# Row-tiled attention scores and maxima on 32 partitions, with another division of the PSUM banks

## The reference

```python
x = x + L0_ffn(L0_cond(x, cond))      # 8 experts of 3 layers, top 2; then attention with 16 heads
                                      # of 4 channels, and 8 experts of 2 layers, top 2
x = x + L1_ffn(L1_cond(x, cond))      # attention with 16 heads of 8 channels; then 16 experts
                                      # with a capacity of 160 rows each, top 2

# the attention of either layer (hd = 4, then 8)
scores = einsum("bhsk,bhtk->bhst", Q, K) / sqrt(hd)
attn = softmax(scores, axis=-1)       # over 512 keys, for each of 16 heads and 512 queries
ao = einsum("bhst,bhtv->bhsv", attn, V)
```

## Time and profile before

| What | Value |
|---|---|
| Median of 3 runs (range) | 543.95 us (543.36 to 544.02) |
| Profiled execution, span | 541.2 us |
| Profiled execution, own time | not listed beside its span; the median is 2.75 us above the span |
| VectorE busy | 315.8 us (58%), 826 instructions |
| ScalarE busy | 278.7 us (51%), 414 instructions |
| GpSimd busy | 136.3 us (25%), 136 instructions |
| Experts A | from about 14 to 136 us |
| Loop of layer 0, first scores to the last values | from 136.4 to about 256 us |
| Loop of layer 1 | from 329.3 to about 456 us |

### The profile page before, as it was taken

How to read it: one execution, slowest core, us unless ns; L and a number is a source line. 1 busy time by engine, 2 the same in 40 slices (tenths; PEclk the granted TensorE clock), 3 DMA queues, 4 the chain that set the end, 5 groups by cost and what they waited for, 6 DMA issues and landing times.

```text
span 541.2 us, 7612 instructions
## 1 busy us (share of the span) xinstructions
PE 494.7 (91%) x2782; PEld 345.1 (64%) x2782; DVE 315.8 (58%) x826; ACT 278.7 (51%) x414; POOL 136.3 (25%) x136
## 2 busy tenths in 40 slices
PE   5899799998989999999999988999999999889980
PEld 4578678886545555554897865445555554669970
DVE  4654444567778787764263577877788663402223
ACT  6734344552546566667454653556656555205640
POOL 5755622331711101200000000101111005231551
PEclk9999899999999999999999998999999999899995
DMA  8970200000700000020000000000000002540003
GB/s 323 303 234 2 78 1 0 1 1 1 307 5 0 1 2 0 1 79 0 2 1 0 1 2 1 1 0 1 0 1 2 0 1 94 249 107 4 19 18 120
DMA packets 12868, 26.57 MB, mean 49 GB/s; under 512 B 1293, under 2 KB 10120, under 8 KB 11808
## 3 DMA queue, kind: packets, MB, share of 16 engines
q1 hardware_dynamic: 11392, 22.91, 12.5%
q0 software_dynamic: 1440, 3.18, 1.9%
HBM read 22.11 MB, written 5.26 MB: 51 GB/s over the span
## 4 chain that ended last, share of the span: by engine, by line
PE 77%; DVE 10%; ACT 5%; issue 3%; DMA 3%; POOL 2%; POOLq 0%; DVEq 0%; SPq 0%; ACTq 0%
PE PS L436 13%; PE PS L468 11%; PE PS L453 10%; PE PS L690 5%; PE PS L579 5%; PE PS L613 5%; PE PS L581 5%; PE PS L580 5%; PE PS L730 3%; PE PS L721 3%; DVE mx L1153 3%; PE PS L342 3%; PE PS L421 2%; PE PS L422 1%; PE PS L443 1%
## 5 line engine op out<-in xcount | busy, mean ns | idle before, releaser
L1153 DVE TENSOR_REDUCE mx<-PS 128x1 f32<-128x512 f32 x256 | 164.6, 685 | 41.8 <-PE PS L436 39.3
L854 ACT ACTIVATE wc_late<-PS 128x1024 f32<-128x1024 f32 x128 | 123.9, 1022 | 62.2 <-PE PS L453 62.0
L436 PE MATMUL PS<-Kp,Qs 128*128 128x512 f32 x256 | 95.9, 438 | 6.9 <-DVE mx L1153 5.2
L436 PEld LDWEIGHTS PS<-Kp,Qs 128*128 128x128 f32 x256 | 44.7, 190 | 70.4 <-DVE mx L1153 40.3
L453 PE MATMUL PS<-Qm,Kp 128*128 128x512 f32 x256 | 75.2, 415 | 0.8 <-DVE Qm L1165 0.6
L468 PE MATMUL PS<-wc_late,v_c 128*16 128x512 f32 x512 | 67.3, 598 | 0.7 <-ACT wc_late L854 0.7
L1438 POOL CAST Kp<-Ks 32x512 fp32r<-32x512 f32 x40 | 24.3, 607 | 135.0 <-ACT Ks L833 133.1
L453 PEld LDWEIGHTS PS<-Qm,Kp 128*128 128x128 f32 x256 | 46.5, 190 | 18.1 <-ACT wc_late L854 3.8
L579 PE MATMUL PS<-wc_late_r 128*128 128x512 f32 x96 | 41.7, 435 | 1.1 <-POOL xT_yT_r L1400 0.6
L1052 DVE TENSOR_SCALAR work<-PS,early 128x512 f32<-128x512 f32 x32 | 22.6, 747 | 25.1 <-PE PS L581 25.1
L954 ACT ACTIVATE work<-PS,late 128x160 f32<-128x160 f32 x64 | 19.8, 396 | 32.5 <-PE PS L721 32.5
(11 more groups left out here) (244 smaller groups left out, 743.5 us busy)
## 6 DMA issues: line engine op xcount, KB each, us to landing
wa<-wa_dram SPq DMA_DIRECT2D x8, 512.0 KB, 9.0
wa<-wc_dram SPq DMA_DIRECT2D x2, 2048.0 KB, 9.8
wc_late<-wc_dram SPq DMA_DIRECT2D x2, 2048.0 KB, 11.1
wb<-wb_dram SPq DMA_DIRECT2D x1, 2048.0 KB, 15.6
sel<-sel_dram POOLq DMA_DIRECT2D x2, 1024.0 KB, 5.6
late<-late_dram SPq DMA_DIRECT2D x1, 1572.0 KB, 14.9
packed_rows<-ao SPq DMA_DIRECT2D x1, 1290.0 KB, 22.9
wb<-packed_rows SPq DMA_DIRECT2D x5, 258.0 KB, 4.3
```

The lines of the kernel that those rows point to most:

```text
L436: filled(mm(p, Qs[:, G % 3, qt * P:(qt + 1) * P], Kp[:, G % 3, j, :], start=True, stop=True), (L, "max", G, qt, j))
L854: A(E4[:, 2 * (i % 2) + jp, :, :], p, ACT.Exp, scale=float(HD[L]) ** -0.5).then_inc(taken[f"s{jp}"], 1)
L1153: V.reduce_max(mx[:, G % 2, qt, j:j + 1], p, AX.X).then_inc(taken[filled_at[key][0]], 1)
```

## The change

Scores and maxima are computed on row tiles of the array: a matmul reads only the 32 partitions of its head's slice, of keys and of queries, with `tile_position=(SL * j, 0)`. So the padded keys `Kp` go, with their clearing, with `place_keys` on GpSimd, with ScalarE's four slices, and with the waits on `Kp_set`. One `Ks` with three buffers takes their place, written by one instruction of ScalarE in every group.

The PSUM slots of the loop change. The maxima get two slots of two banks (`ma`, `mb`), one for each half-set: two matmuls fill it, and one `reduce_max` reads both banks. The scores get two slots of one bank (`sa`, `sb`), used by heads 0 and 2, and by heads 1 and 3. ScalarE's exponentials are one for each head, of 512 columns, four in a step where there were two. The old slots stay for the other stages; `claim` now waits for every slot that shares a bank, if it has been filled since the last such wait.

The order of a step on TensorE becomes: scores of heads 0 and 1, first half-set of maxima, scores of heads 2 and 3, `jobs(L, i, 0)`, second half-set, `values(i - 1)`, `jobs(L, i, 1)`. So the second half-set moves from behind the values to ahead of them.

```diff
-        Kp = sb("Kp", [P, 3, HPG, S], F32R)
-        Ks = sb("Ks", [P, 2, S])
+        Ks = sb("Ks", [P, 3, S], F32R)
...
-        SLOTS = {"m0": (0, 1), "m1": (1, 2), "s0": (2, 4), "s1": (4, 6), "pv": (6, 7), "mi": (7, 8)}
+        SLOTS = {"m0": (0, 1), "m1": (1, 2), "s0": (2, 4), "s1": (4, 6), "pv": (6, 7), "mi": (7, 8),
+                 "ma": (0, 2), "mb": (2, 4), "sa": (4, 5), "sb": (5, 6)}
...
             def claim(key, s):
 
-                if fills[s]:
-                    pe.wait_ge(taken[s], fills[s])
+                a, b = SLOTS[s]
+                for o, (c, d) in SLOTS.items():
+                    if a < d and c < b and cleared.get((s, o), 0) < fills[o]:
+                        pe.wait_ge(taken[o], fills[o])
+                        cleared[s, o] = fills[o]
...
-                def maxima(m, half, slots=("m0", "m1")):
+                def maxima(m, half, slots=None):
...
-                    if qt == 0 and G >= 3:
-
-                        pe.wait_ge(Kp_set, HPG * (L * KEYS + G - 3) + 2 * (half + 1))
+                    if slots is None:
+                        p = claim((L, "max", G, qt, half), "mb" if half else "ma")
+                        for j in range(2):
+                            r = slice(SL * (2 * half + j), SL * (2 * half + j + 1))
+                            last = mm(p[:, j, :], Qs[r, G % 3, qt * P:(qt + 1) * P], Ks[r, G % 3, :], start=True,
+                                      stop=True, tile_position=(SL * (2 * half + j), 0))
+                        filled(last, (L, "max", G, qt, half))
+                        return
                     for j in (2 * half, 2 * half + 1):
                         p = claim((L, "max", G, qt, j), slots[j % 2])
-                        filled(mm(p, Qs[:, G % 3, qt * P:(qt + 1) * P], Kp[:, G % 3, j, :], start=True, stop=True),
-                               (L, "max", G, qt, j))
+                        r = slice(SL * j, SL * (j + 1))
+                        filled(mm(p, Qs[r, G % 3, qt * P:(qt + 1) * P], Ks[r, G % 3, :], start=True, stop=True,
+                                  tile_position=(SL * j, 0)), (L, "max", G, qt, j))
...
-                def scores(i, jp):
+                def scores(i, j):
                     G, kt = divmod(i, TPB)
-                    if kt == 0 and jp == 0:
+                    if kt == 0 and j == 0:
                         wait_taken(pe, (L, "mT", G))
-                    p = claim((L, "s", i, jp), f"s{jp}")
-                    for j in range(2):
-                        last = mm(p[:, j, :], Kp[:, G % 3, 2 * jp + j, kt * P:(kt + 1) * P], Qm[:, G % 2, :],
-                                  start=True, stop=True)
-                    filled(last, (L, "s", i, jp))
+                    p = claim((L, "s", i, j), "sb" if j % 2 else "sa")
+                    r = slice(SL * j, SL * (j + 1))
+                    filled(mm(p, Ks[r, G % 3, kt * P:(kt + 1) * P], Qm[r, G % 2, :], start=True, stop=True,
+                              tile_position=(SL * j, 0)), (L, "s", i, j))
...
                         scores(i, 1)
                         for m in maxima_at(i, 0):
                             maxima(*m)
+                        scores(i, 2)
+                        scores(i, 3)
                         for k in jobs(L, i, 0):
                             job(*k)
+                        for m in maxima_at(i, 1):
+                            maxima(*m)
                         if i:
                             values(i - 1)
-                        for m in maxima_at(i, 1):
-                            maxima(*m)
...
+                def stackK(G):
                     p = wait_full(act, (L, "stack", G, 0))
-                    for j in (2 * half, 2 * half + 1):
-                        r = slice(SL * j, SL * (j + 1))
-                        last = A(Kp[r, G % 3, j, :], p[r, :], ACT.Identity, bias=la("minus")[r, :])
-                    if half:
-                        last.then_inc(taken["mi"], 1)
+                    A(Ks[:, G % 3, :], p, ACT.Identity, bias=la("minus")).then_inc(taken["mi"], 1)
...
-                    p = wait_full(act, (L, "s", i, jp))
-                    A(E4[:, 2 * (i % 2) + jp, :, :], p, ACT.Exp, scale=float(HD[L]) ** -0.5).then_inc(taken[f"s{jp}"], 1)
+                    p = wait_full(act, (L, "s", i, j))
+                    A(E4[:, 2 * (i % 2) + j // 2, j % 2, :], p, ACT.Exp, scale=float(HD[L]) ** -0.5
+                      ).then_inc(taken[filled_at[L, "s", i, j][0]], 1)
...
+                    key = (L, "max", G, qt, half)
+                    if filled_at[key][0] in ("ma", "mb"):
+                        p = wait_full(dve, key)
+                        V.reduce_max(mx[:, G % 2, qt, 2 * half:2 * half + 2], p, AX.X).then_inc(
+                            taken[filled_at[key][0]], 1)
+                        return
...
-            nc.gpsimd.memset(Kp[:, :, :, :].rearrange("p a j s -> p (a j s)").bitcast(F32), 0.0)
...
-            place_keys(0)
```

More of the change, by code:

```diff
@@ L265, in jobs @@
             if place == 0:
-                return {0: [("stackK2", G + 2)] * (more and G > 0), 1: [("stackQ", G + 2)] * more,
-                        2: [("turn", G - 1)] * (G > 0),
+                return {0: [], 1: [("stackQ", G + 2)] * more, 2: [("turn", G - 1)] * (G > 0),
                         3: [("maxT", G + 1)] * (G + 1 < NGB)}[kt]
@@ L283, in build @@
         early_jobs = [{(8, 1): [("cT", 0)], (9, 0): [("qk", 0, 0)], (9, 1): [("v", 0)],
-                       (10, 0): [("stackK", 0), ("stackK2", 0)], (10, 1): [("stackQ", 0)],
-                       (12, 1): [("stackK", 1), ("stackK2", 1)], (13, 1): [("stackQ", 1)],
-                       (14, 1): [("stackK", 2), ("stackK2", 2), ("place", 0)],
+                       (10, 0): [("stackK", 0)], (10, 1): [("stackQ", 0)],
+                       (12, 1): [("stackK", 1)], (13, 1): [("stackQ", 1)],
+                       (14, 1): [("stackK", 2), ("place", 0)],
                        (15, 0): [("maxT", 0), ("max", TPB, 0)], (15, 1): [("max", TPB, 1)]},
                       {(8, 0): [("cT", 0)], (8, 1): [("qk", 0, 0)], (9, 0): [("qk", 0, 1)],
-                       (9, 1): [("stackK", 0), ("stackK2", 0)], (10, 1): [("stackQ", 0)], (11, 0): [("v", 0)],
-                       (11, 1): [("stackK", 1), ("stackK2", 1)], (12, 1): [("stackQ", 1)], (13, 0): [("tanh", 0)],
-                       (13, 1): [("stackK", 2), ("stackK2", 2)], (14, 1): [("place", 0), ("coh", 0)],
+                       (9, 1): [("stackK", 0)], (10, 1): [("stackQ", 0)], (11, 0): [("v", 0)],
+                       (11, 1): [("stackK", 1)], (12, 1): [("stackQ", 1)], (13, 0): [("tanh", 0)],
+                       (13, 1): [("stackK", 2)], (14, 1): [("place", 0), ("coh", 0)],
                        (15, 0): [("maxT", 0), ("max", TPB, 0)], (15, 1): [("max", TPB, 1)]}]
@@ L349, in keep_warm @@
                 pe.wait_ge(taken["m0"], fills["m0"])
+                pe.wait_ge(taken["ma"], fills["ma"])
                 for _ in range(n):
-                    mm(ps("m0"), Qs[:, 0, 0:P], Kp[:, 0, 0, :], start=True, stop=True)
+                    mm(ps("m0"), Qs[:, 0, 0:P], Ks[:, 0, :], start=True, stop=True)
             def field(step):
@@ L463, in values @@
                     p = ps("pv")
-                    for jp in range(2):
-                        wait_taken(pe, (L, "s", i, jp))
+                    for j in (HPG - 2, HPG - 1):
+                        wait_taken(pe, (L, "s", i, j))
                     for j in range(HPG):
@@ L534, in job @@
                         maxima(*at)
-                    elif name not in ("stackK2", "place"):
+                    elif name != "place":
                         {"y": y_, "logits": logits, "count": count, "weightsT": lambda b: weightsT("b", b),
@@ L883, in job @@
                 def job(name, *at):
-                    if name in ("stackK", "stackK2"):
-                        stackK(at[0], int(name == "stackK2"))
+                    if name == "stackK":
+                        stackK(*at)
                     elif name in ("cT", "qk", "tanh", "coh", "stackQ", "aoT", "proj", "logits", "count"):
@@ L891, in main @@
                     for i in range(STEPS):
-                        exps(i, 0)
-                        exps(i, 1)
+                        for j in range(HPG):
+                            exps(i, j)
                         for k in jobs(L, i, 0):
@@ L1157, in place @@
                         dve.wait_ge(clear0, 1)
-                    for j in (HPG - 2, HPG - 1):
+                    for j in (HPG - 2, HPG - 1) if G < 1 else (0, 1):
                         wait_taken(dve, (L, "max", G, TPB - 1, j))
@@ L1430, in part_mla @@
                 nc.gpsimd.tensor_tensor(mla_low[:, m], mlaT[:, m], mla_high[:, m], ALU.subtract).then_inc(mla_split, 1)
-            def place_keys(L):
-                for G in range(3, NGB):
-                    wait_taken(pool, (L, "stack", G, 0))
-                    for j in range(HPG):
```

(5 more changed lines are left out.)

16 lines of the change are left out of this document (4 added, 12 removed).

## The result

The changed kernel takes 684.89 us, the median of 4 runs (679.29 to 690.52), against 543.99 us: a ratio of 1.254, with a 95% interval of 1.247 to 1.261. The ratio leaves out the slowest of the four; the median of the other three is 682.57. The kernel is slower by 141 us. The forecast was slower, by 32 us, within 549 to 600 us. The direction was right and the size was wrong by more than four times.

The account below looks back on a forecast made before the run. TensorE was taken as the bound. Loop steps at +0.49 us each (+20.6), last steps +8, other jobs +2.6, expert stages +2.5 and an absorbed wait -2 made +31.7, so 576 us, range 549 to 600.

Parts of the forecast that it names:

- The large term: Loop scores: heads 2 and 3 wait for exponentials of heads 0 and 1; first score to TensorE free, 2.03 us.
- A stack's copy on ScalarE: In a group's last step, ScalarE must finish this copy before the first exponential: 0.14 us added.
- The bare step: An attention-loop step without stack, turn or transposed maxima: 3.33 us on TensorE, against 3.03 before.
- The changes of mode: TensorE switching between row tiles and the whole array: 0.20 us each way, with 0 as the other end.
- Rival B: On TensorE, the change between row tiles and whole array is free: 549 us, chance 0.12.
- C: On TensorE, row tiles do not run together, so the second pair of maxima costs 0.46 us: 593 us, chance 0.09.
- Rival E: In the loop, the exponential's round trip is as short as 1.33 us, making the kernel faster: 531 us, chance 0.08.
- The sum: Loop steps, last six steps, other jobs, expert stages and an absorbed wait: 20.6 + 8 + 2.6 + 0 + 2.5 - 2 = +31.7 us.
- rival D: Idle TensorE in the loop falls to 1.2 GHz, one stretch in each of 16 groups: +27, 603 us, chance 0.09.

Follow-up runs that it names:

- e7: The kernel before with row tiles for the scores alone, whole-array maxima kept: 537.25 us, ratio 0.987.
- e2: The kernel before with the change's slots, step order, exponentials per head and paired maxima, but whole-array matmuls: 576.88 us, ratio 1.059.
- e4: The changed kernel with one whole-array matmul that nobody reads before head 2, in the 52 steps with a second half-set: 670.01 us.
- e9: The kernel before with row-tiled scores alone, all four matmuls on head 0's partitions, one row group: 569.86 us, ratio 1.050.
- e10: The kernel before with the change's slots, order and four exponentials, row tiles for scores alone, whole-array maxima: 605.67 us, ratio 1.109.
- e11: The kernel before with row tiles for the scores alone, measured again in five rounds: 538.24 us, ratio 0.989.

## Why the prediction was wrong

**The large term was right in kind.** The forecast put the interval from a first score to TensorE free at 2.03 us; the chain has 2.31 (183.31 to 185.62). The exponential is 0.60 where 0.61 was said. A stack's copy on ScalarE, priced at 0.14 in the sum, stands ahead of the first exponential here (183.41). The other 0.14 is a term that was too small: heads 2 and 3 took 0.98, and 0.50 + 0.34 = 0.84 was said. The bare step came closer than that, 3.46 where 3.33 was said, because what follows was shorter: from the end of the maxima (185.85) to the next score (186.77) it is 0.92, and 1.07 was said. The changes of mode were put at 0.20 each, from a column-tiled neighbour, and the stack and the maxima behind it show 0.20. With the Trainium skill's rule (TensorEngine Tiling (Array Packing), Tiling Modes, Key Properties), that a change of mode drains TensorE, the trace agrees for row tiles too. Rival B, that they are free, is out; so is C, since the tiles do overlap.

**Rival E** is out as well. Nothing shortened the round trip. The 3.07 times that the Trainium skill gives for four row tiles (TensorE: Matmul & The Clock Gate, Measured speedup vs the span model) was not reached in this kernel: e7 has 0.44 against 0.92, a factor of 2.1, with a change of mode within it.

**The step that failed is the clock.** The sum ran the whole new step at the upper level, with nothing for the clock, and left it to rival D, which was wrong in its chance (0.09), its price (+27 us) and its reason. The forecast said "If each of 16 groups drew one such stretch": 16 stretches of 3.4 us. There were 292 us in all, five times the 55, and they cost 90 to 108 us (0.31 to 0.37 a us; D took 0.5). It looked for the cause in idle time and argued "most steps would still be 80% busy"; in the loops of the changed kernel TensorE's busy share is 92% by the windows (84% in the stretch at the full clock from 183.50 to 190.10), e2, with the same slots and the whole array, kept the clock, and e4, with row tiles and less idle time than e2, did not. The row that it rested on the earlier trace rows showed a fall after an idle stretch, and I took idleness for the only cause. "Only 32 rows work in its tiles" stood in the text as an aside, and the row tiles were what mattered: without them the same slots give 577 us (e2), near the forecast, though by luck: whole passes for the maxima stand in place of changes of mode. That the clock fell because few rows were at work at a time is the reading that fits best; only e9 against e7 (27 and 7 low us) and the last steps of e10 speak for it directly.

**The sum without the clock** can't be judged as finely. By the two estimates above, 33 to 51 us are left where 31.7 were said. The one term that shows is the 0.98 for heads 2 and 3 in place of 0.84, up to 9 us over 64 steps; e2's chain has 0.98 as well, and e2's expectation, built on the same 2.03, was too low by 7 us or more. e10 has whole-array maxima, row-tiled scores and 51 low us (16 us at 0.31), which leaves 45. No other term was found.

## What to carry to other kernels

Row tiles pay where all the tiles of a set start together in banks that are free together; then four 32-row matmuls are short and the clock stays up (1.1% faster in e11; the rest of what they saved went to waits for VectorE's maxima and to changes of mode). Used singly or in pairs, beside waits, they cost the clock here, and its price (90 to 108 us) dwarfs the passes that they save. So when a change makes the array's tiles smaller, price the kernel at the lower clock too; and when a slot is halved, ask who must release it before the same step can go on.

## What the runs showed of the hardware that was not expected

- TensorE's clock fell to its lower level for 77% of the loops while the engine was 92% busy and no wait of TensorE for the exponentials was longer than 0.8 us, once all of a step's score and maxima matmuls ran singly or in pairs on 32 rows each.
- Row tiles alone cost 96 low us and the new slots alone 6, and both together 292. How the chip weighs rows and idle time is not settled: a whole-array filler that cut TensorE's idle time for exponentials from 28.6 to 11.2 us left 250, and moving the values into the waits (5.6 us of idle time) left 132.
- With row-tiled scores, singly and in pairs, beside whole-array maxima the clock stayed at 0.98 or above in steps 5 to 25; in the steps without maxima it was 0.65 and 0.66 (e10).
- Four row tiles in four banks took 0.51 us from the first start to the last end, and the same four in one row group 1.19 us.
